# Attention scores by 32-row matmul tiles in four shared banks, in place of a block-diagonal key tile

## What is computed

```python
# layer 0, for each graph
nx = layer_norm(x) * g1 + b1
q, k, v = nx @ wq + bq, nx @ wk + bk, nx @ wv + bv          # 8 heads of 32
scores = q @ k.T / sqrt(32) + where(adj > 0, 0.1 * adj * adj, -inf)
x1 = x + softmax(scores) @ v @ wo + bo
x = x1 + gelu(layer_norm(x1) @ w1 + b1) @ w2 + b2           # hidden width 1024
# layer 1, for each graph
q, k, v = x @ Wq + bq, x @ Wk + bk, x @ Wv + bv
h = softmax(where(adj == 0, -inf, q @ k.T / sqrt(32))) @ v @ Wo + bo
x = layer_norm(h + x) * gamma + beta
```

## Time and profile before

| | us |
|---|---|
| median of three runs | 2441.3 (2436.63 to 2442.53) |
| the profiled execution, its own time | 2440.06 |
| its span, first to last instruction | 2438.0 |
| PE busy | 2349.0 (96%) |
| DVE busy | 2027.8 (83%) |
| ACT busy | 1625.3 (67%) |
| POOL busy | 1123.4 (46%) |
| one turn of the loop (steps 5 to 4) | 73 |

### The profile page before, as it was taken

The page is one execution under the profiler, slowest core; times in us unless marked ns, Lnnn a source line. Parts: engine busy times, 40 slices in busy tenths (PEclk is TensorE's granted clock), DMA queues, the critical chain, the costliest instruction groups (busy, mean ns, idle before and its releaser), DMA issues.

```text
span 2438.0 us, 54364 instructions
## 1 busy us (share of the span) xinstructions
PE 2349.0 (96%) x17728; PEld 2000.6 (82%) x17728; DVE 2027.8 (83%) x8620; ACT 1625.3 (67%) x5518; POOL 1123.4 (46%) x1160
## 2 busy tenths in 40 slices
PE   5799999999999999999999999999999999999996
PEld 4688888888888888888888888888888888888875
DVE  4688888888888888888888888888888888888884
ACT  2467666777666777666767666767666767666764
POOL 2245454454454454454454454454454454454454
PEclk8899999999999999999999999999999999999998
DMA  4122212232212222212232212222222222222211
GB/s 128 35 72 64 70 47 60 77 79 64 70 47 62 74 79 64 70 49 66 68 79 64 70 50 65 68 79 64 70 53 61 68 79 64 72 55 58 59 49 42
DMA packets 172630, 159.39 MB, mean 65 GB/s; under 512 B 16832, under 2 KB 168000, under 8 KB 172352
## 3 DMA queue, kind: packets, MB, share of 16 engines
q1 hardware_dynamic: 172352, 155.91, 24.0%
HBM read 55.20 MB, written 16.78 MB: 30 GB/s over the span
## 4 chain that ended last, share of the span: by engine, by line
PE 69%; DVE 24%; issue 3%; ACT 2%; POOL 0%; POOLq 0%; DVEq 0%; ACTq 0%
PE p_bank L1025 37%; PE p_scores L1025 14%; DVE hidden L838 8%; PE p_probs L1113 7%; PE p_bank L1127 6%; DVE hidden L836 5%; PE p_bank L1043 4%; DVE x_two L704 3%; DVE scores L789 2%; ACT scores L592 1%; DVE heads_t L859 1%; ACT heads_t L629 1%; DVE queries_a L813 1%; DVE probs_t L852 1%; DVE res_c L870 1%
## 5 line engine op out<-in xcount | busy, mean ns | idle before, releaser
L542 POOL TENSOR_TENSOR scores<-scores,inverse 128x512 f32<-128x512 f32 x512 | 540.9, 1059 | 729.3 <-DVE inverse L799 729.2
L592 ACT ACTIVATE scores<-scores,negmax 128x128 f32<-128x128 f32 x2048 | 792.6, 391 | 24.0 <-DVE negmax L789 20.2
L1025 PE MATMUL p_bank<-w_down,hidden 128*128 128x256 f32 x3072 | 397.2, 286 | 13.7 <-DVE hidden L838 13.7
L1025 PEld LDWEIGHTS p_bank<-w_down,hidden 128*128 128x128 f32 x3072 | 377.7, 191 | 35.0 <-DVE hidden L838 26.2
L592 ACT ACTIVATION_READ_ACCUMULATOR scores<-scores,negmax 128x1 f32 x2048 | 388.2, 190 | 0.0
L1025 PE MATMUL p_bank<-normed,w_up 128*128 128x512 f32 x1536 | 366.7, 395 | 1.9 <-DVE normed L809 1.9
L1025 PEld LDWEIGHTS p_bank<-normed,w_up 128*128 128x128 f32 x1536 | 285.3, 189 | 61.1 <-issue 2.1
L629 ACT ACTIVATE heads_t<-p_bank 128x256 fp32r<-128x256 f32 x256 | 98.6, 385 | 340.2 <-PE p_bank L1127 340.2
L617 ACT ACTIVATE hidden_raw<-p_bank,ready_cols 128x512 f32<-128x512 f32 x256 | 176.8, 691 | 209.7 <-PE p_bank L1025 112.0
L1113 PE MATMUL p_probs<-ident,scores 128*128 128x128 f32 x2048 | 272.6, 276 | 2.4 <-POOL scores L542 2.4
L1113 PEld LDWEIGHTS p_probs<-ident,scores 128*128 128x128 f32 x2048 | 228.2, 141 | 32.3 <-issue 19.8
(11 more groups left out here) (111 smaller groups left out, 3970.7 us busy)
## 6 DMA issues: line engine op xcount, KB each, us to landing
key_blocks<-hidden SPq DMA_DIRECT2D x512, 128.0 KB, 2.4
x_in<-in_x SPq DMA_DIRECT2D x32, 512.0 KB, 4.5
res_a<-in_x SPq DMA_DIRECT2D x32, 512.0 KB, 4.0
res_c<-x_two SPq DMA_DIRECT2D x32, 512.0 KB, 3.4
out<-res_c SPq DMA_DIRECT2D x128, 128.0 KB, 1.8
adj_a<-in_adj SPq DMA_DIRECT2D x32, 256.0 KB, 3.7
adj_c<-in_adj SPq DMA_DIRECT2D x32, 256.0 KB, 3.2
res_c<-in_L_gnn_w SPq DMA_DIRECT2D x1, 512.0 KB, 5.8
```

The costliest lines, as they stand in the source:

```text
L542: nc.gpsimd.tensor_tensor(rows_c, rows_c, inverse[:, k % 2, heads].unsqueeze(2).broadcast_to([P, HC, P]), ALU.mult).then_inc(probs_made, 1)
L592: last = nc.scalar.activation(scores[:, k % 2, h], scores[:, k % 2, h], ACT.Exp, scale=-1.0, bias=negmax[:, k % 2, h:h + 1], accum_out=tot ...
L1025: last = nc.tensor.matmul(dst, stationary(i), moving(j), start=(n == 0), stop=(n == total_n - 1))
```

## The change

The keys stay in the projection's own layout (features by tokens) in tiles of their own for each stage, as the queries do: `keys_a`, `keys_c`. `key_blocks`, its zero fill, `load_blocks`, `copied` and their semaphores are gone. A head's scores are a matmul of its own: 32 rows (the head's features, on partitions 32j to 32j+31) by 128 stationary columns (queries) by 128 moving columns (keys). Row tiles at different partitions write to different banks: head j of each half goes to bank j of the new `p_heads` (four banks), half c to columns c x 128 on. A unit's scores are 24 matmuls in place of six, with one signal at the end instead of two. The turned probs lie in the upper halves of the same four banks, half c in banks 2c and 2c+1.

Since scores and turned probs share banks, three waits on PE change: S waits for all masks of the unit before and for the copies of the turned probs of the step before; T waits for all masks of the unit scored in the same step. DVE, ACT and POOL keep their order.

```diff
+        keys = {"A": sb("keys_a", [P, 2, KC, TOK], F32R), "C": sb("keys_c", [P, 2, KC, TOK], F32R)}
-        key_blocks = sb("key_blocks", [P, KC, 2, HC, TOK], F32R)
-        keys = hidden[:, FC - KC:FC, :, :]
...
-        p_scores = ctx.enter_context(nc.psum_tensor("p_scores", [P, KC, HC * P], F32))
-        p_probs = ctx.enter_context(nc.psum_tensor("p_probs", [P, KC, HC * P], F32))
+        p_heads = ctx.enter_context(nc.psum_tensor("p_heads", [P, HC, 2 * KC * P], F32))
...
+        def score_columns(c, j):
+            return p_heads[:, j, c * P:(c + 1) * P]
+        def turned_columns(c):
+            return p_heads[:, 2 * c:2 * c + 2, KC * P:2 * KC * P]
...
-            nc.gpsimd.memset(key_blocks[:, :, :, :, :].bitcast(F32), 0.0).then_inc(zeroed, 1)
...
-                        if kind == "K":
-                            copied(act, t, what)
...
-                nc.scalar.activation(probs_t[:, 0:HC].rearrange("p h n -> p (h n)"), p_probs[:, 0, :], ACT.Copy
-                                     ).then_inc(turned_out0, 1)
+                nc.scalar.activation(turned_rows(0), turned_columns(0), ACT.Copy).then_inc(turned_out0, 1)
...
-                dve.wait_ge(scores_made, u * KC + c + 1)
+                dve.wait_ge(scores_made, u + 1)
...
                 if b == 0:
                     for i in range(KC):
-                        bank, number = t.bank(("Q", stage, i), earlier=(stage == "C"))
-                        pe.wait_ge(drained[bank], number)
-                if b % 2 == 0:
-                    pe.wait_ge(blocks_loaded[stage][b // 2], (t.group(s.steps.index(k)) + 1) * HC * 16)
+                        for kind in "KQ":
+                            bank, number = t.bank((kind, stage, i), earlier=(stage == "C"))
+                            pe.wait_ge(drained[bank], number)
+                wait(pe, masked_made, u * H)
+                turns = u if k == s.steps[0] and s.before is not None and s.before.drain else u - 1
+                wait(pe, turned_out0, turns)
+                wait(pe, turned_out1, turns)
+                tokens = slice(b * P, (b + 1) * P)
+                passes = ((HI, HI), (HI, LO), (LO, HI))
                 for c in range(KC):
-                    wait(pe, masked_made, u * H - H + HC * (c + 1))
-                    moving = lambda j: key_blocks[:, c, j, :, b * P:(b + 1) * P]
-                    stationary = lambda i: queries[stage][:, i, c, b * P:(b + 1) * P]
-                    three_passes(p_scores[:, c, :].rearrange("p (h n) -> p h n", h=HC), [(stationary, moving)]
-                                 ).then_inc(scores_made, 1)
+                    for n, (i, i2) in enumerate(passes):
+                        for j in range(HC):
+                            rows_j = slice(HD * j, HD * (j + 1))
+                            last = nc.tensor.matmul(score_columns(c, j), queries[stage][rows_j, i, c, tokens],
+                                                    keys[stage][rows_j, i2, c, tokens], start=(n == 0),
+                                                    stop=(n == len(passes) - 1))
+                last.then_inc(scores_made, 1)
...
                 if op == "T":
+                    scored = u + 1 if r == len(t.s.order) - 1 and t.s.drain else u + 2
+                    pe.wait_ge(masked_made, scored * H)
                     for c in range(KC):
...
-                            last = nc.tensor.transpose(p_probs[:, c, h * P:(h + 1) * P], scores[:, par, HC * c + h, :],
-                                                       ident[:, :])
+                            last = nc.tensor.transpose(turned_columns(c)[:, h // 2, (h % 2) * P:(h % 2 + 1) * P],
+                                                       scores[:, par, HC * c + h, :], ident[:, :])
```

More of the change, by code:

```diff
@@ L266, in build @@
         adj_loaded = {"A": sem("adj_a_loaded"), "C": sem("adj_c_loaded")}
-        blocks_loaded = {n: [sem(f"blocks_{n.lower()}_loaded{i}") for i in range(2)] for n in "AC"}
         stored = sem("stored")
@@ L333, in build @@
         assert len(pieces) == len(staged) == len(piece_loaded)
-        ZEROED = 4
+        ZEROED = 3
         EARLY_VECTOR = 7
@@ L357, in setup_over, with turned_rows @@
                     eng.wait_ge(drained[bank], number)
[L359 to L365, removed]
+        def score_columns(c, j):
+            return p_heads[:, j, c * P:(c + 1) * P]
+        def turned_columns(c):
+            return p_heads[:, 2 * c:2 * c + 2, KC * P:2 * KC * P]
+        def turned_rows(c):
+            return probs_t[:, HC * c:HC * (c + 1)].rearrange("p (a h) n -> p a (h n)", a=2)
         def split_part(kind, stage, part, c):
-            return queries[stage][:, part, c, :] if kind == "Q" else keys[:, c, part, :]
+            return (queries if kind == "Q" else keys)[stage][:, part, c, :]
         shapes = make_shapes()
@@ L415, in drained_use @@
                 return drained[bank], number
[L417 to L424, removed]
             def store(t, b):
@@ L433, in body @@
                 unit0 = t.grown(s.unit0, len(s.order))
-                if s.before is None:
-                    load_blocks("A", 0, drained_use(t, ("K", "A", 1)))
-                    load_blocks("A", 1, drained_use(t, ("K", "A", 1)))
                 if s.a and s.following:
@@ L445, in body @@
                         load_piece(n)
[L446 to L450, removed]
                 if s.m:
@@ L464, in body @@
                     store(t, 2)
-                if s.m:
-                    load_blocks("C", 0, drained_use(t, ("K", "C", 1)))
                 if s.c:
@@ L470, in body @@
                 if s.m:
-                    load_blocks("C", 1, (masked_made, (unit0 + len(s.order)) * H) if s.a
-                                else drained_use(t, ("K", "C", 1)))
                     if s.c:
@@ L491, in _ @@
             nc.gpsimd.memset(half[:, :], -0.5).then_inc(zeroed, 1)
-            nc.gpsimd.memset(key_blocks[:, :, :, :, :].bitcast(F32), 0.0).then_inc(zeroed, 1)
-            pool.wait_ge(zeroed, 3)
+            pool.wait_ge(zeroed, 2)
             nc.gpsimd.affine_select(out=ident[:, :], in_=ident[:, :], compare_op=ALU.not_equal, fill=1.0,
@@ L789, in mask_scores @@
                     nc.vector.tensor_tensor_reduce(
-                        out=scores[:, k % 2, h], in0=p_scores[:, c, (h % HC) * P:(h % HC + 1) * P],
+                        out=scores[:, k % 2, h], in0=score_columns(c, h % HC),
                         in1=adj[stage][:, b, :], scale=1.0, scalar=LARGEST, op0=ALU.add, op1=ALU.min,
@@ L832, in evacuate @@
                         j = use[1]
-                        if j == FC - KC:
-                            copied(dve, t, "M")
                         dve.wait_ge(drained[bank], number)
@@ L851, in turned @@
                 dve.wait_ge(probs_turned, u * KC + 2)
-                nc.vector.tensor_copy(probs_t[:, HC:H].rearrange("p h n -> p (h n)"), p_probs[:, 1, :]
-                                      ).then_inc(turned_out1, 1)
+                nc.vector.tensor_copy(turned_rows(1), turned_columns(1)).then_inc(turned_out1, 1)
             def heads_low(t, r):
```

## The result

| | us | ratio to before |
|---|---|---|
| before, median (2436.63 to 2442.53) | 2441.18 | 1 |
| after, median (2798.07 to 2799.86) | 2799.15 | 1.147, 95% interval 1.145 to 1.149 |
| forecast | 2725 (2620 to 2870) | |

The change costs 358 us. The way, the place and the range were forecast right; the point was 74 us short, and all of that is one term, the clock.

A forecast was written before the change was run, and what follows sets the result against it. It took PE, busy 96%, as the bound, with every added wait lost at once: 2440 + 214 (waits less shorter scores) + 70 (clock) - 1 (copies) = 2723, stated as 2725 us, range 2620 to 2870.

The forecast's parts named there:

- the clock: Half clock on PE after idle gaps in steps 0, 3 and 5: 2.25 us a turn, +70 us, ends 0 and 158.
- S: A unit's scores on PE: 0.95 us (ends 0.75 and 2.6), a gain of 0.5 us a step.
- rivals 1 and 2: Scores on PE: 128 columns cost more, 2800 us (0.2); row tiles don't run together, 3025 us (0.11, with long low clock).
- The wait of T: PE's transposes of the previous unit's probs wait for DVE's masks: net +6.9 us a turn, +214 us.
- steps 0 and 5: Steps opening with transposes of normalised rows, with K products; the masks' wait costs +1.93 us each, hiding the faster scores.
- steps 1, 2, 6 and 7: Steps with a Q or V projection in halves: +0.56 us each; sign: over 1 us idle before the probs' transposes.
- step 3: Step with the up projection and half of the down projection: +1.35 us from the masks' wait.
- The copies: The 512 SyncE copies, the zero fill and their waits go: a gain of 1 us.
- rival 3: The clock holds in the loop: 2653 us; part of the forecast's own range, within its 0.65.
- rival 4: Faster: DVE masks early enough that the probs' transposes never wait in seven steps, 3.6 us a turn won, 2328 us; 0.02.

The follow-up runs named there:

- the run with the clock held: Changed kernel with ten idle 512-column matmuls ahead of the transposes of the probs in steps 0, 3 and 5: 2653.8 us, ratio 1.087.
- late T: Changed kernel with the transposes of the probs moved on PE behind the output product in every step of the loop: 2580.8 us, ratio 1.057.
- the wait alone: Kernel before, with only the wait of the probs' transposes for all eight masks of the unit just scored added: 2828.3 us, ratio 1.159.

## Why the prediction was right, and where it was short

**The bound.** Right. PE's list set the end, and a wait put into it counted in full; DVE, at 83%, was the engine waited for.

**S.** Taken 0.95 us, measured 0.82 and 0.11 to 0.18 for the way in: 0.93 to 1.0. The nearest row was V's, four tiles every 0.11 us. That rate holds here: the doubled scores took 1.49 instead of 0.82 us, so a set of six rounds costs 0.67, 0.11 a round. The forecast had 0.12 for it, and 0.2 for the changes of shape, where 0.15 on the way out to V and 0.11 to 0.18 on the way in were measured; the two misses partly cancel, which is luck. Both dearer bounds (T's rate one after another, V's price for a whole head) are out, and so are rivals 1 and 2. The Trainium skill, TensorE: Matmul & The Clock Gate, "What overlaps and what doesn't", ties the overlap of loads to different row groups; the trace agrees for the passes-outermost order. Head by head, where neighbours in program order mostly share a row group, S took 0.84 us, where by that rule it would have been slower. The measurement decides: in this kernel the order in the program did not matter. The run does not show by what means.

**The wait of T.** Taken +6.9 us a turn, 214 us; with the clock out of the way 213 us were measured, and each kind of step came within 0.2 us. That both ends of each chain were read from the trace (V to the last mask, XT to the last mask) made this term good: none of it rests on the unknown price of S. Doubling S showed that for steps 0 and 5. One sign was a little off: the idle time in front of T in steps 1, 2, 6 and 7 is 0.87 to 0.89 us, where "over 1 us" was said. T does start 1.06 us later after V than before; but the profile counts idle time from the end of the last matmul's latency, and before, T started while that latency still ran.

**The clock.** The step that failed: "half of the three gaps at 1.5 us: 2.25 us a turn, +70 us". It measured 145 us, 4.7 a turn. Both factors were low. First the same gap of step 3 in two turns that follow each other, each with T and the product behind it; then the stretches around the first of them and around the gap of step 0:

```profile
1200.08 1.97 PE L1092 MATMUL p_heads<-ident,scores 128*128 128x128 f32 x8 [2.67 <-DVE negmax L762]
1201.70 4.96 PE L995 MATMUL p_bank<-normed,w_up 128*128 128x512 f32 x12
...
1285.74 1.09 PE L1092 MATMUL p_heads<-ident,scores 128*128 128x128 f32 x8 [2.67 <-DVE negmax L762]
1286.58 3.01 PE L995 MATMUL p_bank<-normed,w_up 128*128 128x512 f32 x12
```

```profile
1197.00:1200.00 3.00, 0.41 (x16) 0.14 (x8) 2.86 (x22) 0.38 (x1) 0.00 (x0) 0.85 0.02 5
1200.00:1203.00 3.00, 2.92 (x11) 2.73 (x12) 1.04 (x4) 1.75 (x2) 1.46 (x2) 0.50 0.35 102
1203.00:1206.00 3.00, 3.00 (x8) 2.33 (x8) 0.59 (x2) 0.82 (x2) 0.00 (x0) 0.51 0.09 29
...
1258.00:1260.00 2.00, 0.00 (x0) 0.00 (x0) 2.00 (x17) 1.59 (x8) 0.00 (x0) 1.00 0.12 31
1260.00:1262.00 2.00, 1.58 (x9) 1.58 (x9) 0.54 (x5) 2.00 (x12) 1.04 (x1) 0.63 0.72 240
1262.00:1264.00 2.00, 2.00 (x7) 1.61 (x6) 0.78 (x2) 0.46 (x1) 0.78 (x1) 0.51 0.00 0
```

After the first gap T takes 1.62 us to the next product, after the second, of the same length, 0.84: the clock doesn't fall every time. Nor does each fall cost the same: at 1200 it is low for over 6 us, twice what the earlier trace rows had shown, at 1260 for 3.4. So one turn proves little; here are the 25 turns (26 for step 5) of PE's timeline from 200 to 2350 us:

| step | no fall | fall, +1.6 us | fall, +2.7 us |
|---|---|---|---|
| 5 | 0 (9.4 us) | 26 (10.9 to 11.0) | 0 |
| 0 | 8 (9.4) | 9 (11.0) | 8 (12.1) |
| 3 | 9 (24.0) | 8 (25.6) | 8 (26.7) |

That is 59 falls after 76 gaps, 2.3 a turn where half of three was taken, and 1.9 us for each in the mean where 1.5 was taken: 4.4 us a turn in the loop. I had priced a fall by the single one that I read, and its chance by feeling, though my own argument (the gap is emptier than that stretch) spoke for more than half. The upper end of that term, 158 us, was close. What decides which gap is followed by a fall stays open.

**The copies.** Counted at 1 us. 2440 + 214 - 1 is the 2653 of rival 3, and the run with the clock held gave 2653.8, so nothing larger shows there; the copies by themselves were not tried. The DMA queue's share fell from 24% to 10%, and PE had waited only 0.9 us for them.

**Faster.** The condition of rival 4 (the masks end before T in seven steps) could be met by moving T, which the diff didn't do. Its price, 3.6 us a turn, did not come through even with the readers' queues put in order: 1.0 did, since the next waits stand close behind.

## What to carry to other kernels

When two results are made to share a bank, list each new wait and measure in the old trace from the event that starts its chain to the event that ends it: the stall is that length less the work in between, and a faster producer ahead of the chain doesn't shorten it. Price gaps on TensorE twice, once as idle time and once for the half clock that follows; filling the three gaps of a turn (2.4 to 2.7 us) with useless matmuls won 5% here. Read the clock over many turns: in this kernel one and the same gap was followed by three different outcomes. A product moved to a later place needs its evacuations moved in the readers' queues as well.

## What the runs showed of the hardware

- 32-row tiles of float32r with 128 columns run four at a time at the rate of V's 32-column tiles, 0.11 us for four: 24 in 0.82 us up to V's start, 48 in 1.49, where six matmuls of 512 columns took 1.45.
- A change from whole-array matmuls into 32-row tiles cost 0.18 us behind XT (0.97 instead of 0.79) and 0.11 behind a projection (1.49 instead of 1.38).
- Single gaps of 0.9 us (steps 1, 2, 6 and 7) left the clock at its upper level; but where one of 0.86 was followed by three of 0.45 (late T, step 3) it fell in 17 of 28 turns.
- A gap of 1.82 us (scores twice, steps 0 and 5) was followed by T and K at full speed 51 times of 51; gaps of 1.86 to 1.89 (the wait alone) by a fall 12 times of 51; one of 2.44 (changed kernel) 43 of 51; one of 2.67 (step 3) 16 of 25 in the changed kernel, 23 of 25 with the wait alone and 25 of 25 with the scores twice. So the length of the gap alone did not decide.
